# Attention value products issued in pairs of groups instead of one by one

## The reference

```python
x = x + tanh(g_xattn[0]) * L0_xattn(layernorm(x), ctx, ctx)   # decayed running sum of ctx*ctx, times layernorm(x)
x = x + tanh(g_ffn[0])   * L0_ffn(layernorm(x), ...)          # gate/up/down, FP4 block quantised, silu
x = x + tanh(g_xattn[1]) * L1_xattn(layernorm(x), ctx, ctx, 16)
x = x + tanh(g_ffn[1])   * L1_ffn(layernorm(x), ...)          # block floating point, gelu
```

```python
q, k = rope(q), rope(k)
scores = einsum('bqhd,bkhd->bhqk', q, k) / sqrt(hd) + alibi_bias
out = einsum('bhqk,bkhd->bqhd', softmax(scores), v)
```

## Time and profile before

| | us |
|---|---|
| three runs | 857.71, 859.51, 860.60 |
| median | 859.51 |
| the profiled execution | 860.34 |
| its span in the profile | 858.2 |
| busy: PE, DVE, ACT, POOL | 713.5, 708.5, 488.0, 431.1 |

### The profile page before, as it was taken

How to read it: one execution, slowest core, us unless ns; L and a number is a source line. 1 busy time by engine, 2 the same in 40 slices (tenths; PEclk the granted TensorE clock), 3 DMA queues, 4 the chain that set the end, 5 groups by cost and what they waited for, 6 DMA issues and landing times.

```text
span 858.2 us, 16571 instructions
## 1 busy us (share of the span) xinstructions
PE 713.5 (83%) x5090; PEld 517.0 (60%) x5090; DVE 708.5 (83%) x1230; ACT 488.0 (57%) x939; POOL 431.1 (50%) x331
## 2 busy tenths in 40 slices
PE   2255999999999998779999999999999775777775
PEld 1255888887888877556565555656565333444444
DVE  6867788998889887868898989898888658888885
ACT  3433545445454342337777777777778674555553
POOL 4524565555655545644444554555443526655553
PEclk8576999999999999879999999999999987888898
DMA  8800000000000000010000000000001000100011
GB/s 279 246 3 0 1 1 1 0 0 0 0 0 1 1 1 1 1 50 2 3 2 2 1 1 1 2 1 1 1 1 50 2 1 1 37 25 24 26 37 50
DMA packets 17719, 18.35 MB, mean 21 GB/s; under 512 B 1670, under 2 KB 16912, under 8 KB 17680
## 3 DMA queue, kind: packets, MB, share of 16 engines
q1 hardware_dynamic: 17084, 17.66, 6.4%
q10 hardware_dynamic: 596, 0.20, 0.1%
HBM read 13.39 MB, written 4.19 MB: 20 GB/s over the span
## 4 chain that ended last, share of the span: by engine, by line
PE 33%; DVE 30%; issue 16%; POOL 9%; ACT 8%; DVEq 1%; DMA 1%; POOLq 1%; ACTq 0%; SPq 0%
PE a_ps_t L561 7%; PE a_ps_m L579 6%; DVE maxima L1497 5%; PE a_ps_pv L615 4%; DVE f_ps_small L1582 4%; PE a_ps_s L600 3%; POOL hs L1110 3%; PE ps_o L522 3%; DVE hup L1324 2%; DVE f_hcode L1598 2%; DVE yup L1293 2%; POOL xres L1090 2%; DVE hscale L1318 2%; ACT hmag L866 1%; PE a_ps_pv L623 1%
## 5 line engine op out<-in xcount | busy, mean ns | idle before, releaser
L1497 DVE TENSOR_REDUCE maxima<-a_ps_m 128x2 f32<-128x512 f32 x256 | 166.3, 687 | 35.4 <-PE a_ps_m L579 34.7
L919 ACT ACTIVATE probs<-a_ps_s 128x512 f32<-128x512 f32 x256 | 149.2, 602 | 42.3 <-PE a_ps_s L600 40.1
L579 PE MATMUL a_ps_m<-stack_t 64*128 64x256 f32 x512 | 107.5, 328 | 19.9 <-DVE maxima L1497 16.7
L579 PEld LDWEIGHTS a_ps_m<-stack_t 64*128 64x128 f32 x512 | 68.3, 188 | 78.7 <-DVE maxima L1497 49.5
L600 PE MATMUL a_ps_s<-stack_t 64*128 64x256 f32 x512 | 100.0, 308 | 3.7 <-ACT probs L919 2.9
L1141 POOL TENSOR_TENSOR stack<-roped,stack 128x512 f32<-128x512 f32 x32 | 42.6, 1333 | 116.8 <-DVE stack L1487 115.3
L491 PE MATMUL ps_gu<-w1h,yth 128*128 128x352 f32 x256 | 88.6, 346 | 13.2 <-DVE h L1311 13.2
L522 PE MATMUL ps_o<-w2t,hqt 128*128 128x256 f32 (+1 forms) x384 | 97.9, 390 | 0.2 <-ACT hqt L851 0.2
L615 PE MATMUL a_ps_pv<-probs,v_aug 128*32 128x256 f32 x1024 | 83.0, 396 | 2.9 <-ACT probs L919 2.5
L910 ACT CAST stack_t<-a_ps_t 128x512 fp32r<-128x512 f32 x128 | 70.9, 588 | 24.5 <-PE a_ps_t L561 23.7
L561 PE MATMUL a_ps_t<-idf,stack 128*128 128x128 f32 x512 | 77.2, 294 | 9.0 <-POOL stack L1141 4.6
(11 more groups left out here) (176 smaller groups left out, 1613.3 us busy)
## 6 DMA issues: line engine op xcount, KB each, us to landing
xres<-in_x SPq DMA_DIRECT2D x16, 256.0 KB, 3.2
ctx<-in_ctx SPq DMA_DIRECT2D x16, 256.0 KB, 3.8
out_x<-f_y SPq DMA_DIRECT2D x16, 256.0 KB, 2.1
w1a_raw<-in_w_gate_up SPq DMA_DIRECT2D x1, 1024.0 KB, 6.2
w_raw<-in_w_fc SPq DMA_DIRECT2D x1, 1024.0 KB, 5.7
w_raw<-in_w_proj SPq DMA_DIRECT2D x1, 1024.0 KB, 5.0
w_raw<-in_w_down SPq DMA_DIRECT2D x1, 704.0 KB, 9.3
stack_t<-neg_max_t SPq DMA_DIRECT2D x32, 8.0 KB
```

Of the source, the lines that this page charges most:

```text
L579: ins = nc.tensor.matmul(a_ps_m[:, half, n, :], a_stack_t[b.par][rows, 0, pair, c * P:(c + 1) * P], a_stack_t[b.par][rows, 1, pair, :], st ...
L919: nc.scalar.activation(a_probs[:, u % 8], a_ps_s[:, u % 2], ACT.Exp).then_inc(a_exp, 1)
L1497: nc.vector.tensor_reduce(a_maxima[:, b.par, c, 4 * quad + half:4 * quad + half + 3:2], a_ps_m[:, half], X, ALU.max).then_inc(a_v_max, 1)
```

## The change

On PE, inside the loop over m, two value groups are issued one behind the other whenever the number of score groups issued so far is 6, 10 or 14, in place of one at each even number from 4 on. The last two groups are both issued behind the loop; in the last body they both stand behind the two FFN products. The groups, their operands, their semaphore waits and the other engines' lists are the same.

```diff
@@ at_body (PE)
                     if m % 8 != 7:
                         at_scores(b, u)
                         u += 1
-                        if u % 2 == 0 and u >= 4:
+                        if u % 4 == 2:
+                            at_times_v(b, (u - 6) // 2)
                             at_times_v(b, (u - 4) // 2)
                     if not nxt and m == 8:
                         turn_w34(2)
@@
                     ff_fc(lead[0], 0)
                     ff_fc(lead[0], 1)
+                at_times_v(b, PG - 2)
                 at_times_v(b, PG - 1)
                 if nxt:
                     at_turn_max(nxt)
```

## The result

The changed kernel takes 893.39 us (median of 6, 889.77 to 894.77), the kernel before 860.06 (6 runs, 857.1 to 861.08): ratio 1.0386, 95% interval 1.0354 to 1.0417. Slower was forecast, but 883.3 in a range of 871 to 892; the measured time lies 1.4 us outside. The profiled execution took 889.92, with a span of 887.8, 29.6 more than before. M, S, V, T are the groups of the prediction's first paragraph.

What follows compares the result with a forecast made beforehand. PE and VectorE, each waiting for the other in a ring, were taken as the bound. 15 bodies at 1.52 us (22.8) plus 1.0 for the last body made 23.8, so 883.3 us on the median, range 871 to 892.

Steps and rivals of the forecast that it cites:

- The ring: Attention loop: max products and VectorE's reductions wait for each other over two banks; delays above 0.04 us idle VectorE.
- its places: Where pairs cost time in a body: ahead of reductions 4, 9 and 13, and before the turn of the maxima.
- T to T: Sign in the changed trace: 20.9 to 21.3 us from one turn of the maxima to the next.
- the four prices: Extra time per body at the four places: 0.48 + 0.36 + 0.48 + 0.20 = 1.52 us.
- The second V: Second of two adjacent value-product groups on PE: holds it 0.48 us more, own range 0.45 to 0.57.
- The last term: End of a body: value groups 6 and 7 both precede the turn of the maxima, +0.20 us.
- 15 bodies: 22.8 us: Attention loop: 1.52 us more in each of 15 turns, with nothing taking it up.
- The last body: Last turn, without max products: 0.96, say 1.0 us more, bounds 0 to 1.2.
- Its two shifts: Last turn: value group 5's pair delays the turned input, +0.48 us; value group 6 moves behind the first FFN products, +0.48.
- Every second V in full: Rival, chance 0.10: each pair's second value group costs 0.57 us, 2.28 per body, 34.2 in all, giving 893.7 us.
- faster through fewer mode changes: Rival, chance 0.08: PE's own time sets the pace; pairs save 0.18 us each, 10.8 in all, giving 848.7 us.

Runs made afterwards that it cites:

- e6: Kernel before with only value group 2 moved, from behind score group 7 to directly in front of value group 3; 873.68 us, one run.
- e10: Kernel before with the changed kernel's pairs only in the bodies of batches 0, 14 and 15; 870.96 us, ratio 1.0113.
- e8: Changed kernel plus 5 unused products on PE behind each of five max-product groups; 882.54 us, ratio 1.0252 to the kernel before.
- e4: Kernel before with value groups 1 to 5 moved later, 6 and 7 at the end, ACT's copies of sums moved to follow; 866.95 us, ratio 1.0065.

## Why the prediction was wrong, point by point

- *The ring and its places* were right: the gaps came where named, T to T in clean bodies is 20.8 (20.9 to 21.3 was forecast), and the four prices add up. M2 starts 0.06 behind the end of reduction 0 by the rows, not 0.05, which changes nothing in the sum.
- *The second V* was taken at 0.48, from the spacing of two passes that start from rest; it is 0.43, below the own range's lower end of 0.45. By place: 0.43, 0.34, 0.44, 0.06 against 0.48, 0.36, 0.48, 0.20. The last term left out PE's way round the loop. Of the 0.34, a part is a longer gap ahead of reduction 13 (e6), which the prediction did not have. Together 1.27 against 1.52, 3.8 us too many over 15 bodies.
- *The failed step* is "15 bodies: 22.8 us". It took every body at the 2.4 GHz level because rows 2 showed 1.00, and no rival priced a change of it. The stage became 27.5 us longer: 19.2 by the ring and 8.3 by a lower clock, which the new order on PE brings, since the drops in the middle are absent in the kernel before and in e10, and go when the waits are filled in e8. The row was read as a property of the stage; it was a result of the order on PE.
- *The last body* was put at 1.0, in bounds of 0 to 1.2; it was 3.3, and 5.4 in e10. Its two shifts were right in kind (0.48 to 1.74 ahead of f_xt), but with the clock at 0.63 the pairs there hold PE for up to 1.87 in place of 1.00. How the 3.3 divides between the shifts and the clock was not tested.
- *The sum of the miss.* The forecast for the profiled execution was 884.1, and it took 889.92: 3.6 less by the ring, 8.3 more by the clock in the stage, 2.3 more behind it, 1.2 less ahead. The other 4.3 of the 10.1 us between 883.3 and 893.39 lie between the profiled execution and the median.
- *The rivals.* "Every second V in full" gave 893.7, almost the measured time, and is wrong: no place cost 0.57. That it came nearest is luck: too high a price of the ring stood in for the clock. Of "faster through fewer mode changes" the saving is real, 0.14 per pair, but it is saved on a group that cost nothing at its old place.
- *Still open.* The profiled execution has 29.6 of the 33.3 us between the medians. The other runs are up to 4.9 us longer, mostly at a lower mean clock (0.906 to 0.924 against 0.923); drops in more bodies would fit, but there is no trace of them: each kernel has one. What the clock follows on PE is open too: it was tried with more products and with moved ones, not with products of another shape.

## What to carry to other kernels

In a ring of two engines with two buffers, an operation that belongs to neither costs anything from nothing to its whole length, and where it stands decides: look for what the partner does besides (here a rotation and a cast) and put it just ahead of that. Two of them back to back cost once more at each place without cover, however much the pair itself saves. And when PE's order changes, price a fall of the granted clock in every body, the first and last above all: here it was worth more than a quarter of the effect, and it took the gain from two better orders.

## What the runs showed of the hardware

- Eight passes of 128 x 32 matmuls hold PE for 0.57 us, sixteen for 1.00 at the 2.4 GHz level and 1.86 at 1.2 GHz (changed kernel, 397.39).
- In the changed kernel the clock fell at 499.7 us after waits of PE of 0.54 and 0.70 us, no longer ones. In e4 it fell at 530.8 us after PE's row had been busy for 10.51 of 10.8 us. Unused products can raise a kernel's speed: 893.39 to 882.54 us.
- Moving one value group of 0.57 us (e6) came with a drop of the clock in three of the middle bodies, which took 2.1 to 2.4 us more than the others of their kind.
